# One product of Wv and Wout ahead of everything, six tiles of lead for the chain over x, and GpSimd's additions tile by tile

## The reference

```
attention: kv = context @ Wkv; v = second half; a query i sees only the keys j with j % 2048 == i
           (154 keys: query i < 154 gets v[i]; every later query has all keys masked alike,
            and gets the mean of v over the 154 keys)
           x = x + attn @ Wout + bout
ffn:       h = layernorm(layernorm(x)) * gamma + beta
           hq, sx = round(h * 127 / max|h|)                 per row
           w1q, sw = ternary(w1 / mean|w1|)
           h = gelu(hq @ w1q.T / (sx * sw) + b1)            512 -> 2048
           y = quantised in the same way, with w2           2048 -> 512
           x = x + y + b2
```

## Time and profile before

| | before |
|---|---|
| median of 3 runs | 602.17 us |
| the profiled execution's own time | 601.81 us |
| its span, first to last instruction | 600.0 us |
| TensorE matmul busy | 545.9 us (91%) |
| VectorE busy | 458.5 us (76%) |
| ScalarE busy | 423.7 us (71%) |
| GpSimd busy | 378.5 us (63%) |
| DMA | 78.36 MB, mean 131 GB/s |
| mean granted clock of TensorE | 0.986 |

### The profile page before, as it was taken

The page is one execution under the profiler, slowest core; times in us unless marked ns, Lnnn a source line. Parts: engine busy times, 40 slices in busy tenths (PEclk is TensorE's granted clock), DMA queues, the critical chain, the costliest instruction groups (busy, mean ns, idle before and its releaser), DMA issues.

```text
span 600.0 us, 7964 instructions
## 1 busy us (share of the span) xinstructions
PE 545.9 (91%) x2471; PEld 240.5 (40%) x2518; DVE 458.5 (76%) x724; ACT 423.7 (71%) x417; POOL 378.5 (63%) x435
## 2 busy tenths in 40 slices
PE   0999689399999999999999999999999999999997
PEld 0734234144444444444444444444444444444443
DVE  2152763898888888888888888888888888888653
ACT  0034580587888888888888888888888888888862
POOL 3022760877777777777777777777777777777200
PEclk9999799799999999999999999999999999999999
DMA  8990220057765555455555555555555455333422
GB/s 285 400 396 36 57 28 13 11 169 184 198 143 124 123 128 127 122 124 126 129 127 128 128 127 128 127 128 127 128 128 122 119 128 124 89 89 87 106 72 87
DMA packets 136718, 78.36 MB, mean 131 GB/s; under 512 B 113992, under 2 KB 114028, under 8 KB 136676
## 3 DMA queue, kind: packets, MB, share of 16 engines
q1 hardware_dynamic: 133940, 71.04, 46.4%
q10 hardware_dynamic: 2736, 6.82, 3.1%
HBM read 33.53 MB, written 17.00 MB: 84 GB/s over the span
## 4 chain that ended last, share of the span: by engine, by line
DVE 36%; POOL 27%; PE 18%; issue 11%; DMA 3%; ACT 2%; SPq 1%; POOLq 0%; ACTq 0%; DVEq 0%
POOL hx L339 13%; POOL xr L343 7%; DVE xmax L629 6%; DVE hmax L644 6%; DVE xstep L632 6%; DVE hid L640 6%; DVE stat L615 6%; PE py L832 5%; PE p L808 4%; PE p L784 4%; DVE xr L665 3%; POOL var_e L328 3%; POOL rstd L331 2%; PE py L760 2%; DMA hid<-wv_d 2%
## 5 line engine op out<-in xcount | busy, mean ns | idle before, releaser
L808 PE MATMUL p<-w1q,xqT 128*128 128x512 bf16 x995 | 232.4, 384 | 2.9 <-issue 1.9
L832 PE MATMUL py<-w2q,hqT 128*128 128x512 bf16 x1006 | 230.0, 379 | 0.9
L486 ACT ACTIVATE hq<-hid,hscale 128x2048 int8<-128x2048 f32 x64 | 128.2, 2004 | 71.4 <-DVE hscale L650 71.4
L832 PEld LDWEIGHTS py<-w2q,hqT 128*128 128x128 bf16 x1024 | 100.2, 98 | 120.8
L808 PEld LDWEIGHTS p<-w1q,xqT 128*128 128x128 bf16 x1024 | 96.0, 99 | 123.5 <-issue 20.1
L479 ACT ACTIVATE hid<-p,xdeq 128x1024 f32<-128x1024 f32 x128 | 140.5, 1099 | 0.4 <-PE p L808 0.4
L339 POOL TENSOR_TENSOR hx<-hx,beta_b 128x1024 f32<-128x1024 f32 (+1 forms) x33 | 87.8, 2662 | 11.9 <-ACT hx L464 11.9
L324 POOL TENSOR_TENSOR xr<-xr,attn 128x1024 f32<-128x1024 f32 (+1 forms) x33 | 76.5, 2319 | 28.6 <-ACT attn L498 24.8
L328 POOL TENSOR_SCALAR var_e<-mv 128x2 f32<-128x2 f32 x32 | 19.5, 609 | 104.0 <-DVE mv L617 103.8
L640 DVE TENSOR_REDUCE hid<-hid 128x1 f32<-128x1024 f32 x64 | 77.3, 1207 | 8.0 <-ACT hid L479 8.0
L629 DVE TENSOR_REDUCE xmax<-hx 128x2 f32<-128x1024 f32 x32 | 39.0, 1219 | 57.4 <-POOL hx L339 57.4
(11 more groups left out here) (88 smaller groups left out, 347.3 us busy)
## 6 DMA issues: line engine op xcount, KB each, us to landing
xr<-x SPq DMA_DIRECT2D x64, 256.0 KB, 2.9
out<-xr SPq DMA_DIRECT2D x64, 256.0 KB, 2.2
wout<-wout_d ACTq DMA_DIRECT2D x8, 256.0 KB, 8.0
hid<-wv_d SPq DMA_DIRECT2D x8, 256.0 KB, 13.2
raw<-w1T ACTq DMA_DIRECT2D x4, 512.0 KB, 13.6
raw<-w1T SPq DMA_DIRECT2D x4, 512.0 KB, 20.0
xr<-w2T ACTq DMA_DIRECT2D x2, 512.0 KB, 19.5
attn<-w2T SPq DMA_DIRECT2D x2, 512.0 KB, 15.8
```

Source lines behind the costliest of these rows:

```text
L486: nc.scalar.activation(hq8[:, t % 2, :], hid[:, t % 2, 0:HID], ACT.Copy, scale=col(hscale, t))\
L808: mm = nc.tensor.matmul(p1[:, n * D:(n + 1) * D], xT[:, k, :], w1q[:, k, n * D:(n + 1) * D], start=False, stop=(k == KD - 1))
L832: mm = nc.tensor.matmul(py[:, t % 2, :], hqT[:, t % 2, c // 2, c % 2, :], w2q[:, c, :], start=(c == 0), stop=(c == 2 * NJ - 1))
```

## The change

The kernel after is the kernel before with three changes.

1. *Wv times Wout first.* TensorE forms `wvo` = Wv @ Wout (512 x 512) from 8 blocks, into the four banks of `p1`; ScalarE copies it out. The tail rows and means are then ctxt @ wvo (4 products), the main rows ctxm @ wvo (4 products a batch instead of 8). The rows of batches 1, 2 and 3 are formed before FFN1(0), those of batch 0 after it. The DMA order is new: Wv, Wout and w1 first on both queues, then x, the context, b1 and w2; four blocks of w2 land in the place of Wout. b1's rows are made by VectorE from a mask (`bias_rows`), without the 12 small DMAs.
2. *Six tiles of lead.* Statistics are taken for s + 6 and s + 7, one centring moves to the odd step, and each further link of the chain stands in a later step. `hx` holds three pairs. ScalarE rounds x straight into `xq`, GpSimd widens it in place, and `xi` is gone. SyncE transposes s + 1 and s + 2 in the odd step. `xstep` is written by one instruction a column.
3. *Tile by tile.* GpSimd's additions of attention, beta and b2 in the loop work on one tile each.

The core of the diff:

```diff
@@ sync @@
+            load_wv(0)
+            load_wv(1)
+            load_w1(0)
...
+            load_x(0)
+            sp.dma_start(gamma_b[:, :], gamma.partition_broadcast(P)).then_inc(gamma_loaded, 16)
...
+            load_w2(0)
+            load_w2(2)
             load_x(2)
+            load_x(4)
+            sp.wait_ge(wvo_done, KD)
+            for j in range(4, 8):
                 load_w2(j)
...
             transpose_x(0)
             transpose_x(1)
-            transpose_x(2)
-            transpose_x(3)
...
-                if s == 3:
-                    sp.wait_ge(wq_ready[1], 8)
-                    for t in range(8, 14):
+                if s == 0:
+                    sp.wait_ge(wq_ready[1], 4)
+                    for t in range(8, 11):
                         load_x(t)
-                if s >= 3 and live(s + 11):
+                if live(s + 11):
                     load_x(s + 11)
...
                 if s % 2 == 1:
-                    for t in (s + 3, s + 4):
+                    for t in (s + 1, s + 2):
                         if live(t):
                             transpose_x(t)
@@ gpsimd @@
             def add_b2(t):
-                pool.wait_ge(xgamma_done, t + 2)
-                pool.tensor_tensor(xtile(t, 2), xtile(t, 2), b2_b[:, :, :].broadcast_to([P, 2, D]), ALU.add)\
-                    .then_inc(xb_ready, 2)
+                pool.wait_ge(xgamma_done, t + 1)
+                pool.tensor_tensor(xtile(t), xtile(t), b2_b[:, :, :], ALU.add).then_inc(xb_ready, 1)
...
             add_attention(2, 2)
-            inverse_std(2)
+            add_attention(4, 2)
+            inverse_std(2, 2)
             pool.wait_ge(b2_loaded, 16)
             add_b2(0)
+            add_b2(1)
             add_beta(2, 2)
-            add_attention(4, 2)
-            scale_rows(2)
-            widen_x(2, 2)
-            add_b2(2)
+            inverse_std(4, 2)
+            add_attention(6, 2)
+            for t in range(2, 6):
+                add_b2(t)
 
             for s in range(T + LAG):
...
                 if s % 2 == 0:
+                    if live(s + 6):
+                        inverse_std(s + 6, 2)
                     if live(s + 4):
-                        inverse_std(s + 4)
-                        add_b2(s + 4)
-                        add_beta(s + 4, 2)
+                        add_beta(s + 4, 1)
+                        add_beta(s + 5, 1)
+                    if live(s + 2):
+                        scale_rows(s + 2, 2)
+                        widen_x(s + 2, 2)
                 else:
+                    if live(s + 7):
+                        add_attention(s + 7, 1)
+                        add_attention(s + 8, 1)
                     if live(s + 5):
-                        add_attention(s + 5, 2)
-                    if live(s + 3):
-                        scale_rows(s + 3)
-                        widen_x(s + 3, 2)
+                        add_b2(s + 5)
+                        add_b2(s + 6)
@@ scalar @@
+            abs_w1(1, 4)
+            abs_w1(3, 5)
+            abs_w1(5, 6)
+            abs_w1(7, 7)
+            round_weights(0, 1)
+            for m in range(KD):
+                copy_wvo(m)
+            round_weights(0, 3)
+            abs_w2(1, 4)
             act.wait_ge(mean_done, 1)
-            nc.scalar.activation(attn[:, 2, :], pb[:, :], ACT.Copy).then_inc(mean_copied, 1)
+            nc.scalar.activation(attn[:, 2, :], py[:, 1, :], ACT.Copy).then_inc(mean_copied, 1)
+            abs_w2(3, 5)
+            times_std(0)
+            abs_w2(5, 6)
+            times_std(1)
+            abs_w2(7, 7)
+            round_x(0)
+            round_x(1)
+            times_std(2)
+            times_std(3)
+            for j in (1, 3, 5, 7):
+                round_weights(1, j)
             gelu(0, 0)
             gelu(0, 1)
+            times_std(4)
+            times_std(5)
+            round_x(2)
+            round_x(3)
...
                 if s % 2 == 0:
-                    for t in (s + 4, s + 5):
+                    for t in (s + 2, s + 3):
+                        if live(t):
+                            round_x(t)
+                else:
+                    for t in (s + 5, s + 6):
                         if live(t):
                             times_std(t)
@@ vector @@
+                for i in range(t, t + n):
+                    nc.vector.tensor_scalar(col(xstep, i), col(xmax, i), EPS, 1.0 / QMAX,
+                                            ALU.max, ALU.mult).then_inc(xstep_done, 1)
...
-                if s % 2 == 0 and live(s + 4):
-                    for t in (s + 4, s + 5):
-                        statistics(t)
-                    for t in (s + 4, s + 5):
-                        centre(t)
-                if s % 2 == 1 and live(s + 3):
-                    x_scale(s + 3)
+                if s % 2 == 0 and live(s + 6):
+                    statistics(s + 6)
+                    statistics(s + 7)
+                    centre(s + 6)
+                if s % 2 == 1:
+                    if live(s + 3):
+                        x_scale(s + 3, 2)
+                    if live(s + 6):
+                        centre(s + 6)
@@ tensor @@
             for m in range(KI):
                 pe.wait_ge(wv_loaded[m], 16)
+                pe.wait_ge(wout_loaded[m], 16)
+                if m == KI - 1:
+                    pe.wait_ge(const_set, 3)
+                    weight_total(0)
                 for k in range(KD):
+                    mm = nc.tensor.matmul(p1[:, k * D:(k + 1) * D], wv[:, m // 4, m % 4, k * P:(k + 1) * P],
+                                          wout[:, m, :], start=(m == 0), stop=(m == KI - 1))
```

More of the change, by code:

```diff
@@ L31, with block_program @@
 QMAX = 127.0
-def block_program(nc, x, ctxm_d, ctxt_d, wv_d, wout_d, bout, w1T, b1, w2T, b2, gamma, beta, out, tail_rows):
+def block_program(nc, x, ctxm_d, ctxt_d, wvT, wout_d, bout, w1T, b1, w2T, b2, gamma, beta, out, tail_rows):
     es = ExitStack()
@@ L222, in transpose_h @@
                                        hq8[:, t % 2, :].bitcast(I16)).then_inc(hT_landed[t % 4], 16)
[L224 to L227, removed]
+            load_wv(0)
+            load_wv(1)
+            load_w1(0)
+            load_wv(2)
+            load_w1(2)
+            load_wv(3)
+            load_wv(4)
+            load_w1(4)
@@ new lines, in top, with bias_rows @@
+            def top(v):
+                return v.bitcast(BF16).rearrange("p (n two) -> p n two", two=2)[:, :, 1]
+            def bias_rows():
+                dve.wait_ge(row_set, 3)
+                nc.vector.tensor_reduce(row_pick, row_of.rearrange("p (g c) -> p c g", g=4)[:, 0:3, :], AX.X, ALU.add)\
+                    .then_inc(row_picked, 1)
+                dve.wait_ge(row_picked, 1)
+                dve.wait_ge(b1_split, 2)
+                nc.vector.tensor_scalar(b1rows[:, :], top(b1f), row_pick[:, 0:1], None, ALU.mult).then_inc(b1_rows, 1)
+                for a in range(2):
+                    dve.wait_ge(b1_rows, a + 1)
+                    nc.vector.scalar_tensor_tensor(b1rows[:, :], top(b1res[:, a, :]), row_pick[:, a + 1:a + 2],
+                                                   b1rows[:, :], ALU.mult, ALU.add).then_inc(b1_rows, 1)
@@ L758, in out_rows @@
             def out_rows(b, bank):
-                for m in range(KI):
-                    mm = nc.tensor.matmul(bank, vTm[m][:, b * P:(b + 1) * P], wout[:, m, :],
-                                          start=(m == 0), stop=(m == KI - 1))
+                for k in range(KD):
+                    mm = nc.tensor.matmul(bank, ctxm[:, k, b * P:(b + 1) * P], wvo[:, k, :],
+                                          start=(k == 0), stop=(k == KD - 1))
                 mm.then_inc(attn_done, 1)
-            pe.wait_ge(cmean_done, 1)
```

420 lines of the change are left out of this document (185 added, 235 removed).

## The result

The changed kernel takes **586.02 us** (median of 4 runs, 585.01 to 586.49) against 602.04 us for the kernel before beside it: ratio 0.973, interval 0.971 to 0.975. The forecast was 569.0 with a range of 561 to 583; it missed by 17 us, and the time lies outside the range. The profiled execution took 585.01 us, with a span of 583.3.

What follows compares the result with a forecast made beforehand. Bound: VectorE's wait for GpSimd's beta and `xstep` in the loop, plus a long start. Sum: 102.5 + 458.1 + 3.3 + 3 + 1.8 + 0.4 = 569.1 us, 16.8 gained from start, 16.4 from loop; range 561 to 583.

Steps and rivals of the forecast that it cites:

- the wait for beta and then `xstep`: Steady loop: VectorE waits for GpSimd's beta (2.82 us), then `xstep` takes 1.22 us; TensorE loses 0.64 us per two tiles.
- At 1.2 VectorE has 13.7 us, still below 14.68: Steady loop: even if `xstep` stays at 1.2 us, VectorE's load per two tiles remains below TensorE's 14.68 us.
- My sum: Steady loop: VectorE's load per two tiles from the trace: 15.32 less 1.60 waiting and the `xstep` saving, 12.8 us.
- SyncE: Odd step's queue: x transposition issued at 3.5 us, lands 2.6 us later, slack 1.1 us; cost taken as 0.
- 1 us each at most: Steps 5 and 7: three more DMA issues stand ahead of the x transposition, costing this much per step.
- its bound of 18 us: SyncE's queue: worst case, a 4.3 us landing costs 0.6 us per two tiles, times 30.
- step 3: Start: w1's weight scale at about 31 us, tail out at 40, GpSimd's first attention addition at 42.
- The first: Rival: the loop stays bound outside TensorE, the start gains, the 0.64 us stay; 585.5 us, chance 0.09.
- "between" case: Loop: an x transposition late by 0.3 us per two tiles gives 578 us; between forecast and first rival, chance 0.14.
- The second: Rival: the start isn't shortened, FFN1(3) stays at about 118 us, the loop gains; 582 us, chance 0.06.
- third: Rival: GpSimd's six single-tile operations each wait 0.75 us, 16.2 us per two tiles; 611.7 us, chance 0.05.
- The rule on the shared port: Loop: the odd centring waits up to 1.2 us for GpSimd, next GELU moves 0.2 us, the sum by nothing.

Runs made afterwards that it cites:

- e4: The kernel before with only `xstep` written one column at a time: 584.0 us, 0.970 of the kernel before.
- e7: e1 with `xstep` as one instruction of two columns again: 588.49 us, 0.981 of the kernel before.
- e1: The changed kernel with the odd step's x transpositions issued ahead of the load of x and the three tail-spreading DMAs: 571.48 us, 0.949 of the kernel before.
- e6: e1 with w1's scale and first rounding ahead of the context sums in VectorE's queue: 570.34 us, 0.949 of the kernel before.
- e2: The changed kernel with the tail-spreading DMAs in steps 6, 8, 10 and 12 instead of 5 to 8: 577.1 us, 0.958 of the kernel before.
- e3: The changed kernel with GpSimd's additions of attention, beta and b2 in the loop in pairs again: 586.7 us, 0.975 of the kernel before.
- e9: e1 with GpSimd's loop additions in pairs again: 576.32 us, 0.959 of the kernel before.

## Why the prediction was wrong

**The direction and the pace were right, by partly wrong reasons.** 14.68 us per two tiles, 149 ns a column and 1.25 us a beta came as forecast. But the two steps that I named as the bound, the wait for beta and then `xstep`, weren't worth the same: e4 shows that the lead wasn't needed for the pace, e7 that without the short `xstep` it doesn't bring it. "At 1.2 VectorE has 13.7 us, still below 14.68" is false: with the two-column form VectorE takes 15.3 us. My sum added the durations of the kernel before; in the changed order more casts and centrings meet GpSimd's additions, and the sum lacks what they are stretched by.

**The step that failed: "SyncE", valued at 0.** I had the x transposition issued 3.5 us after FFN1, landing in 2.6, and a slack of 1.1 us. Measured, with a step at 311.99:

```profile
313.68 0.34 SPq L259 DMA_DIRECT2D out<-xr  x1
314.13 1.29 SPq L219 DMA_TRANSPOSE hT<-hq  x1
315.47 0.58 SPq L182 DMA_DIRECT2D xr<-x  x1
316.17 2.53 SPq L211 DMA_TRANSPOSE xqT<-xq  x2
```

It is issued at 4.18 us: the store waits for the result until 1.69, and the hidden tile's transposition starts only at 2.14. With a landing of 2.6 to 3.1 us that leaves 0.1 to 0.6 us of slack. That is why steps with three more issues ahead, which I took at "1 us each at most", cost 2.9 us of wait each, and one of them a stretch at the low clock as well. The issues themselves did cost about 1 us; what I had left out is that the landing behind them took 5.0 and 4.7 us. I had found the mechanism, written down its bound of 18 us, and then taken the end of it that was convenient; the landing time of 4.3 us in the earlier trace rows alone said that 1.1 us of slack was not safe. The price measured is 14.5 us (e1), almost the whole miss.

**The start: step 3 failed, the later ones moved with it.** The scale of w1 was at 36.5 us, not 31, since in VectorE's queue it stands behind the context sums, whose last block lands at 34.8; the tail came out at 44.5 (forecast 40), GpSimd's first addition at 47.2 (42), FFN1(0) at 60.9 (56.4), FFN1(1) at 75.7 (71), FFN1(2) at 100.3 (95), FFN1(3) at 107.4 (102.5). Each from the tail on is 4.5 to 5.3 us late: the working between them held. But e6 shows that taking the 4 us back at the scale gives at most 2 at FFN1(3) and 1.1 in the time: the lateness isn't simply passed on.

**The rivals.** None of the three is what happened. The first names the right time (585.5) for another reason; its "between" case, an x transposition that comes late, is the mechanism, priced at 578, though the loss came in four large waits and not evenly. The second and third are out: FFN1(3) moved by 11.9 us, and the loop runs at 14.68 us per two tiles, not 16.2, with GpSimd busy for 83.5% of its time.

**The rule on the shared port.** My text gave it one centring and no effect. The trace shows it in more instructions. GpSimd's timeline beside VectorE's, same kernel:

```profile
300.18 2.96 POOL L319 TENSOR_TENSOR xr<-xr,attn 128x512 f32<-128x512 f32 x2
303.10 2.50 POOL L338 TENSOR_TENSOR xr<-xr,b_b 128x512 f32<-128x512 f32 x2
```

```profile
300.41 1.59 DVE L639 SCALAR_TENSOR_TENSOR hx<-xr,mv,gamma_b 128x512 f32<-128x512 f32 x1
301.92 1.21 DVE L656 TENSOR_REDUCE hid<-hid 128x1 f32<-128x1024 f32 x1
...
304.82 1.33 DVE L672 CAST hqT<-hT 128x1024 bf16<-128x1024 int8 x1
```

The centring started 0.23 us after an addition and took 1.59 us, twice its 0.74; the cast started inside the second b2 addition and ended 0.6 us after it; the reductions kept their 1.21. The Trainium skill, "SBUF — State Buffer", section "Who interferes with whom", names both forms (two SBUF inputs, and casts or `tensor_scalar` in a two-port mode) and exempts `tensor_reduce`; the trace agrees. What I left out is that it adds up: per two tiles 15.3 us instead of 13.7 in e7.

**Open.** The landing of 5.2 us before FFN1(18) came again in e2 (4.9) and e3 (4.7) at the same step, with nothing but the load ahead in the queue. In e1 tile 18's landed in 2.6 us, but that of tile 19, issued right behind it and with a whole step more to spare, took 4.2. It ends in e2 as in the changed kernel, with 1.8 us in which 32 GB/s are moved, so it isn't a queue full of bytes; what holds the last packets wasn't tried. No run has the new start and the short `xstep` without the six tiles of lead, so what the lead is worth by itself isn't measured; it is what took the slack from the x transpositions.

## What to carry over

When a change takes lead away from a transfer, write out the queue that issues it, every entry with what it waits for, and put the transfer with the least slack first; a slack smaller than the spread of landing times in the trace is a cost, not a zero. Before removing a wait, look at what stands right behind it in the same queue: here it was enough to shorten a two-element instruction, and that one line was worth as much as the whole change. Loads of an engine summed from undisturbed durations are a lower bound where two engines hold each other up.

## What the runs showed of the hardware

- A transposition of x landed 2.6 us after issue at best, 5.01 and 4.72 us with a load and three more DMA issues ahead of it on its queue, 5.17 once with the load alone. The DMA share doesn't tell how much is moved: the loop moved 133 GB/s at a share of 0.58, and the last 2 us of that one landing 21 GB/s at 0.54.
- An int8 to bf16 cast of 128x1024 took 0.69 us beside no addition of GpSimd, and 1.82 us on average beside additions of pairs (e9).
- TensorE can pay for a wait twice: after one of 2.89 us FFN1(6) took 5.31 us instead of 3.63, and after one of 2.00 us FFN1(18)'s step was 1.69 us longer than usual, but after one of 2.96 FFN1(8) took its usual 3.63.
- A `tensor_scalar` on two columns took 1.20 us in the median in the kernel before and 0.53 in e7; one on a single column took 0.14 to 0.16 us in all of its 64 cases, in the changed kernel and in e4.
